# An adaLN, attention and mixture-of-experts block: the first large expert tiles are chosen from six batches and loaded ahead of the last sends

## The reference

```python
h = layernorm(x) * (1 + ca) + sa
x = x + ga * attention(h)             # exp(tanh(scores * 1/distance)), rows normalised
h = layernorm(x) * (1 + cb) + sb
logits = h @ Wg
top_v, top_i = top_k(logits, 2);  w = softmax(top_v)
sparse = sum over the two chosen e of  w_e * (relu(h @ W1[e] + b1[e]) @ W2[e] + b2[e])
shared = relu(h @ Ws1 + bs1) @ Ws2 + bs2
x = x + gb * (sparse + shared)
```

## Time and profile before

| | us |
|---|---|
| median of 3 runs | 648.14 (645.54 to 649.86) |
| profiled execution, its own time | 647.72 |
| its span | 646.0 |
| busy: PE / DVE / ACT / POOL | 609.2 / 461.2 / 402.3 / 345.7 |
| chain that ended last, PE's share | 66% |
| chain that ended last, POOL `rows_x` L577 | 5% |

### The profile page before, as it was taken

How to read it: one execution, slowest core, us unless ns; L and a number is a source line. 1 busy time by engine, 2 the same in 40 slices (tenths; PEclk the granted TensorE clock), 3 DMA queues, 4 the chain that set the end, 5 groups by cost and what they waited for, 6 DMA issues and landing times.

```text
span 646.0 us, 13359 instructions
## 1 busy us (share of the span) xinstructions
PE 609.2 (94%) x4311; PEld 555.7 (86%) x4311; DVE 461.2 (71%) x1403; ACT 402.3 (62%) x643; POOL 345.7 (54%) x341
## 2 busy tenths in 40 slices
PE   3898999999999998989988999999999999999995
PEld 2586988898889897878978999999999999999995
DVE  7889879798989898986812676765555445453788
ACT  3588787878787866567444556565555656555541
POOL 4531614766666666768660566666555556556000
PEclk9999999999999999989998999999999999999998
DMA  7140000111111111111256566666666666601972
GB/s 292 43 164 2 1 1 10 37 34 35 32 37 35 34 34 35 40 47 39 96 176 202 162 181 189 188 179 207 193 204 188 184 195 190 203 30 34 361 307 114
DMA packets 29885, 76.44 MB, mean 118 GB/s; under 512 B 7126, under 2 KB 11374, under 8 KB 29712
## 3 DMA queue, kind: packets, MB, share of 16 engines
q1 hardware_dynamic: 20480, 58.49, 28.1%
q0 software_dynamic: 8640, 16.93, 7.7%
q10 hardware_dynamic: 720, 0.47, 0.2%
HBM read 53.53 MB, written 23.24 MB: 119 GB/s over the span
## 4 chain that ended last, share of the span: by engine, by line
PE 66%; DVE 17%; POOL 7%; issue 6%; ACT 3%; DMA 1%; POOLq 0%; DVEq 0%; ACTq 0%; SPq 0%
PE value L1918 21%; PE value L1738 11%; PE score L1710 9%; PE score L1712 8%; PE score L1711 8%; POOL rows_x L577 5%; DVE rows_all L1168 2%; DVE stats L1039 2%; DVE rows_all L1155 2%; PE value L1969 2%; DVE work L1146 2%; PE misc L1751 2%; PE misc L1918 1%; PE misc L1693 1%; POOL rstd L557 1%
## 5 line engine op out<-in xcount | busy, mean ns | idle before, releaser
L745 POOL DMA_INDIRECT rows_z<-tile_y,tags x138 | 143.0, 1036 | 110.4 <-DVE tile_y L1535 49.7
L1710 PE MATMUL score<-h_hi,h_lo 128*128 128x512 f32 (+1 forms) x252 | 93.8, 372 | 2.5 <-DVE h_hi L1249 1.8
L1738 PE MATMUL value<-w_ring,work 128*128 128x129 f32 x768 | 93.6, 279 | 2.0 <-ACT work L805 1.9
L1738 PEld LDWEIGHTS value<-w_ring,work 128*128 128x128 f32 x768 | 91.2, 195 | 4.3 <-ACT work L805 2.6
L932 ACT ACTIVATE work<-score,w_ring 128x512 f32<-128x512 f32 (+1 forms) x96 | 53.1, 615 | 58.7 <-PE score L1712 57.1
L1712 PE MATMUL score<-h_hi,h_lo 128*128 128x512 f32 (+1 forms) x252 | 88.7, 352 | 0.0
L1711 PE MATMUL score<-h_hi,h_lo 128*128 128x512 f32 (+1 forms) x252 | 88.3, 351 | 0.0
L803 ACT ACTIVATE work<-work 128x1024 f32<-128x1024 f32 x64 | 67.2, 1050 | 26.9 <-DVE work L1146 26.7
L577 POOL DMA_INDIRECT rows_x<-work,slot x64 | 64.7, 1011 | 35.8 <-issue 17.7
L1146 DVE TENSOR_TENSOR work<-score,lw 128x1024 f32<-128x1024 f32 x64 | 76.5, 1214 | 1.8 <-PE score L1712 1.2
L1918 PE MATMUL value<-w_ring,work 128*128 128x128 f32 x640 | 75.4, 275 | 0.0
(11 more groups left out here) (253 smaller groups left out, 1216.3 us busy)
## 6 DMA issues: line engine op xcount, KB each, us to landing
w_ring<-packs SPq DMA_DIRECT2D x24, 578.0 KB, 3.8
rows_all<-packs SPq DMA_DIRECT2D x23, 578.0 KB, 3.9
lw<-rows_x SPq DMA_DIRECT2D x24, 260.0 KB, 3.6
res<-x SPq DMA_DIRECT2D x8, 512.0 KB, 5.9
h_t<-rows_z SPq DMA_DIRECT2D x3, 1024.0 KB, 9.9
mod<-mod_rows SPq DMA_DIRECT2D x1, 2560.0 KB, 10.0
rows_z<-tile_y,tags POOLq DMA_INDIRECT x142
rows_all<-rows_z SPq DMA_DIRECT2D x2, 1024.0 KB, 12.5
```

Of the source, the lines that this page charges most:

```text
L745: nc.gpsimd.indirect_dma_start(rows_z[:, :], bass.IndirectOffsetOnAxis(ap=tags[pos][:, k, 0:1].bitcast(I32), axis=0), tile_y[par][:, k, :] ...
L1710: nc.tensor.matmul(out, a_lo, b_hi, start=True, stop=False)
L1738: ins = nc.tensor.matmul(value[:, s // 3, c0:c0 + D + 1], prob[:, t % 4, s * P:(s + 1) * P], normal[b % 3][:, t, :], start=(t == 0 and s % ...
```

## The change

The first three large tiles of the table (positions 0, 2 and 4 of the first cycle) are always tiles of one expert: the one with most rows in batches 0 to 5. Three tiles are 1536 rows, which that expert has in these batches in any case, as 12288 rows go to 8 experts. `first_tiles`, ten small DVE instructions, picks it, fills the three entries and raises `first_ready`; the rest of the table is computed later for 21 large tiles, with that expert's region starting 1536 rows further and its count 1536 lower (one instruction more in `total_counts`). The number of tiles stays.

```diff
+            def first_tiles():
+                step = Chain(dve, chosen_step, 0)
+                step(nc.vector.tensor_tensor(count[:, :], place[:, 0, :], region_at[:, :], ALU.subtract))
+                step(nc.vector.max(first_v[:, :], count[:, :]))
+                step(nc.vector.max_index(first_i[:, :], first_v[:, :], count[:, :]))
+                step(nc.vector.tensor_copy(first_f[:, :], first_i[:, 0:1]))
+                step(nc.vector.tensor_tensor(first_hot[:, :], expert_no[:, 0, :], first_f[:, :].to_broadcast([P, E]), ALU.is_equal))
+                step(nc.vector.tensor_tensor(own_at[:, :], first_hot[:, :], region_at[:, :], ALU.mult))
+                step(nc.vector.tensor_reduce(first_r[:, :], own_at[:, :], AX.X, ALU.add))
+                step(nc.vector.tensor_copy(table_e[:, 0:RING, 0], first_f[:, :].to_broadcast([P, RING])), wait=False)
+                step(nc.vector.scalar_tensor_tensor(out=own_at[:, :], in0=first_hot[:, :], scalar=float(RING * TILE), in1=region_at[:, :],
+                                                    op0=ALU.mult, op1=ALU.add), wait=False)
+                nc.vector.tensor_scalar(table_r[:, 0:RING, 0], tile_no[:, 0:RING, 0], float(TILE), first_r[:, 0:1],
+                                        ALU.mult, ALU.add).then_inc(first_ready, 1)
+                dve.wait_ge(first_ready, 1)
+                dve.wait_ge(chosen_step, step.now())
```

DVE calls it between `split_x` of tile 3 and `last_rows`, and takes the `split_x` of tile 6 ahead of `small_tiles`:

```diff
             split_x(3, 1, shared_rows(3))
+            first_tiles()
             last_rows()
...
             large_tiles()
+            split_x(6, 0, shared_rows(6))
             small_tiles()
             small_table()
-            split_x(6, 0, shared_rows(6))
             split_x(7, 1, shared_rows(7))
```

SP loads W0 and W2 at `first_ready`, and R0 and R2 when the sends of six batches have landed, ahead of its wait for `counted` and of the pads; behind them only W1 and R1 are left:

```diff
+            sp.wait_ge(first_ready, 1)
+            for pos in range(0, RING, 2):
+                load_weights(pos, pos)
+            for par in range(2):
+                sp.wait_ge(scattered[par], 16 * 2 * G * FIRST_SENT // 2)
+            for pos in range(0, RING, 2):
+                load_rows(pos, pos)
+
             sp.wait_ge(counted, 1)
...
-            sp.wait_ge(large_table_ready, 1)
-            for pos in range(0, RING, 2):
-                load_weights(pos, pos)
             sp.wait_ge(table_ready, 1)
-            for pos in range(1, RING, 2):
-                load_weights(pos, pos)
-            rows_at = [first_row(pos, pos) for pos in range(RING)]
+            load_weights(1, 1)
+            row_at_1 = first_row(1, 1)
             sp.wait_ge(padded, 16 * (E + 1))
             for par in range(2):
                 sp.wait_ge(scattered[par], 16 * 2 * G * B // 2)
-            for pos in range(RING):
-                load_rows(pos, pos, rows_at[pos])
+            load_rows(1, 1, row_at_1)
```

PE's order becomes D5, U7, T0, D6, V0, wait `counted`, first half of D7, T1, second half of D7, T2, and then the loop as before:

```diff
             shared_up(7)
-            shared_down(6)
-            pe.wait_ge(counted, 1)
...
             transpose_rows(0, 0, True)
-            shared_down(FRONT - 1)
-            transpose_rows(0, 1, True)
+            shared_down(FRONT - 2)
             expert_up(0, 0)
+            pe.wait_ge(counted, 1)
+            shared_down(FRONT - 1, lambda: transpose_rows(0, 1, True))
             transpose_rows(0, 2)
```

ACT follows: the split of W0 comes ahead of `relu(7)`, the split of R0 ahead of the evacuation of D6, and that of D7 behind the split of R1:

```diff
             evacuate_shared(5)
-            relu(7, w_shared, 1)
-            evacuate_shared(6)
...
             expert_w(0, 0)
+            relu(FRONT - 1, w_shared, (FRONT - 1) % 2)
             expert_x(0, 0)
-            evacuate_shared(FRONT - 1)
+            evacuate_shared(FRONT - 2)
+            expert_relu(0, 0)
             expert_w(0, 1)
             expert_x(0, 1)
-            expert_relu(0, 0)
+            evacuate_shared(FRONT - 1)
             expert_w(0, 2)
```

More of the change, by code:

```diff
@@ L65 @@
 AHEAD = 3 + (B - 2) // 2
+FIRST_SENT = B - 2
+assert RING * TILE * E <= 2 * S * FIRST_SENT
+assert (LARGE_TILES - RING) * TILE <= 2 * T - RING * TILE - E * (TILE - 1) + TILE - 1
 assert LARGE_TILES * TILE <= 2 * T - E * (TILE - 1) + TILE - 1
@@ L209, in adaln_moe @@
         rest = sb("rest", [P, E])
+        first_v = sb("first_v", [P, E])
+        first_i = sb("first_i", [P, E], U32)
+        first_f = sb("first_f", [P, 1])
+        first_hot = sb("first_hot", [P, E])
+        first_r = sb("first_r", [P, 1])
+        own_at = sb("own_at", [P, E])
         count_i = sb("count_i", [P, E], I32)
@@ L326, in adaln_moe @@
         counted = sem("counted")
+        chosen_step = sem("chosen_step")
+        first_ready = sem("first_ready")
         large_table_ready = sem("large_table_ready")
@@ L1429, in tiles_up_to, with fill_table @@
                 return sum_of[3]
-            def fill_table(kind, ends, size, limit):
+            def first_tiles():
[14 more added lines that the diff above has]
+                dve.wait_ge(chosen_step, step.now())
+            def fill_table(kind, ends, size, limit, first=0):
                 tables(nc.vector.scalar_tensor_tensor(out=row_at[:, 0:E], in0=ends[:, before_], scalar=-float(size), in1=row_at[:, 0:E],
@@ L1435, in fill_table @@
                 tables(nc.vector.tensor_tensor(row_step[:, :], row_at[:, 1:E + 1], row_at[:, 0:E], ALU.subtract))
[L1437 to L1447, removed]
+                n = LARGE_TILES - first
+                ends_b = ends[:, own].rearrange("p (o e) -> p o e", o=1).to_broadcast([P, n, E])
+                step_b = row_step[:, :].rearrange("p (o e) -> p o e", o=1).to_broadcast([P, n, E])
+                tables(nc.vector.tensor_tensor(past[:, 0:n, :], tile_no[:, 0:n, :], ends_b, ALU.is_ge))
+                tables(nc.vector.tensor_reduce(tile_e[:, 0:n], past[:, 0:n, :], AX.X, ALU.add), wait=False)
+                tables(nc.vector.tensor_scalar(tile_r[:, 0:n], tile_no[:, 0:n, 0], float(size), row_at[:, 0:1], ALU.mult, ALU.add))
+                tables(nc.vector.tensor_scalar(table_e[:, first:, kind], tile_e[:, 0:n], float(E - 1), None, ALU.min), wait=False)
+                tables(nc.vector.tensor_tensor(past[:, 0:n, :], past[:, 0:n, :], step_b, ALU.mult))
+                tables(nc.vector.tensor_reduce(tile_e[:, 0:n], past[:, 0:n, :], AX.X, ALU.add))
+                tables(nc.vector.tensor_tensor(tile_r[:, 0:n], tile_r[:, 0:n], tile_e[:, 0:n], ALU.add))
+                return (nc.vector.tensor_scalar(table_r[:, first:, kind], tile_r[:, 0:n], float(limit), None, ALU.min))
             def total_counts():
@@ L1454, in total_counts @@
                 nc.vector.tensor_tensor(pad_at[:, :], count[:, :], region_at[:, :], ALU.add).then_inc(counted, 1)
+                dve.wait_ge(counted, 1)
+                tables(nc.vector.scalar_tensor_tensor(out=count[:, :], in0=first_hot[:, :], scalar=-float(RING * TILE), in1=count[:, :],
+                                                      op0=ALU.mult, op1=ALU.add))
             def large_tiles():
                 ends = tiles_up_to(0, count, TILE, 0)
-                tables(nc.vector.tensor_scalar(ends[:, own], ends[:, own], float(LARGE_TILES), None, ALU.min), wait=False)
-                tables(nc.vector.tensor_copy(row_at[:, 0:E], region_at[:, :]), wait=False)
+                tables(nc.vector.tensor_scalar(ends[:, own], ends[:, own], float(LARGE_TILES - RING), None, ALU.min), wait=False)
+                tables(nc.vector.tensor_copy(row_at[:, 0:E], own_at[:, :]), wait=False)
                 tables(nc.vector.memset(row_at[:, E:E + 1], float(SPARE)))
-                fill_table(0, ends, TILE, SPARE).then_inc(large_table_ready, 1)
+                fill_table(0, ends, TILE, SPARE, RING).then_inc(large_table_ready, 1)
                 dve.wait_ge(large_table_ready, 1)
                 tables(nc.vector.tensor_tensor(rest[:, :], ends[:, own], ends[:, before_], ALU.subtract))
-                tables(nc.vector.scalar_tensor_tensor(out=row_at[:, 0:E], in0=rest[:, :], scalar=float(TILE), in1=region_at[:, :],
+                tables(nc.vector.scalar_tensor_tensor(out=row_at[:, 0:E], in0=rest[:, :], scalar=float(TILE), in1=own_at[:, :],
                                                       op0=ALU.mult, op1=ALU.add), wait=False)
@@ L1908, in up, with down @@
                         ins.then_inc(up_ready, 1)
-            def down(n, w, bank, part, rows=TILE, first=False, banks=2):
+            def down(n, w, bank, part, rows=TILE, first=False, banks=2, halfway=None):
                 if not first:
@@ L1913, in down @@
                 for c in range(C):
+                    if halfway and c == PART:
+                        halfway()
                     if c % PART == 0:
@@ L1925, in shared_up, with shared_down @@
                 up(n, 0, n % 2, 0, first=(n == 0))
-            def shared_down(n):
-                down(n, w_shared, yacc[n % 2], n % 2, first=(n < 2))
+            def shared_down(n, halfway=None):
+                down(n, w_shared, yacc[n % 2], n % 2, first=(n < 2), halfway=halfway)
             def total_ranks():
```

## The result

The changed kernel takes 641.16 us (median of 5 runs, 640.41 to 642.41), the kernel before 647.41 (median of 5, 645.54 to 649.86): ratio 0.9911, 95% interval [0.9893, 0.9928], so 5.8 us less by the ratio. The profiled execution took 641.10 against 647.72, its span is 639.3 against 646.0. The forecast was 640.9. The change is real, but by the bound of 1% it falls into "within 1%", which I had given 0.43, and not into "faster by over 1%", to which I gave 0.53. The first four experiments (e1 to e4) fell in a time in which the kernel before took 674.8 us beside them, 28 more than otherwise, and why is open.

What follows compares the result with a forecast made beforehand. PE bounds the kernel, full in the expert loop with one idle hole ahead. Gains 6.75 + 0.65 - 0.24 = 7.16, taken as 7.2, off the profiled 647.72 give 640.5, or 640.9 against the median 648.14; range 638.8 to 645.0 us.

Steps and rivals of the forecast that it cites:

- within 1%: Total time: outcome that the change differs from the kernel before by less than 1% (6.5 us); chance 0.43.
- faster by over 1%: Total time: outcome below the 641.7 us line; chance 0.53, of which 0.50 forecast's case and 0.03 rivals.
- PE's order and the early loads: PE ahead of the expert loop: the same work without a wait takes 25.11 instead of 31.86 us, 6.75 gained.
- The low clock: PE behind its idle hole: first transposes and the `down` after them at low clock cost 1.73 us, part of 6.75.
- The loss in V1 and E0: Second expert `up` follows the first before ACT's ReLU is through: 5.70 instead of 5.22 us, 0.48 lost.
- `split_x` of tile 6: DVE: moved ahead of `small_tiles`, this split lets PE's `up` of tile 6 start at 323.48, 0.65 us gained.
- `first_tiles` at nothing: DVE: ten added instructions take 1.7 to 2.35 us and fit in 2.52 idle ahead of `last_rows`, costing nothing.
- the sends beside it would grow: Two sends beside `first_tiles` each grow by 0.98, together 2.0 us; part of a rival with chance 0.18.
- R1: Second tile's row load, behind the last send: its transposes on PE wait 0.24 us, range none to 1.5.
- R1 or the sends come late: Rival, ahead of the loop: late sends or row loads cut the gain to 4.1 or about 5.5 us; chance 0.18.
- the likeliest case: Total time: the forecast holds, with gains of 6.6 to 7.5 us, 639.0 to 642.7 with runs' spread; chance 0.67.
- Three quarters beyond the line: Share of the forecast's own case put past the 1% line at 641.7 us, giving 0.50.

Runs made afterwards that it cites:

- e1: Kernel before with only PE's and ACT's new order, first row load still behind all sends; ratio 1.0012, beside a kernel before at 674.8 us.
- e4: Kernel before with 38 useless matmuls filling PE's idle time ahead of the wait; ratio 1.013, beside a kernel before at 674.8 us.
- e2b: Changed kernel with PE's and ACT's order of the kernel before, early loads kept, second measurement; 641.18 us, ratio 0.9913 to the kernel before.
- e1b: Kernel before with only PE's and ACT's new order, no early loads, second measurement; 650.90 us, ratio 1.0061 to the kernel before.
- e4b: Kernel before with 38 useless matmuls filling PE's idle time ahead of the wait, second measurement; 649.65 us, ratio 1.0044.
- e6: Changed kernel with `split_x` of tile 6 moved back behind `small_table`; 640.49 us, ratio 0.9908 to the kernel before.
- c_after: Changed kernel measured again without any edit, as yardstick; 640.03 us, ratio 0.9907 to the kernel before.
- e5: Changed kernel with the second tile's transposes behind three quarters of the `down` around them instead of half; 640.18 us, ratio 0.99.
- e7: Changed kernel with one more POOL instruction, a useless power, ahead of the last three sends; 641.23 us, ratio 0.991 to the kernel before.
- e8: Changed kernel with 128 no-effect waits (64 instructions) on PE near the start, shifting its later code; 641.31 us, ratio 0.9915.

## Why the prediction was right

- **PE's order and the early loads (6.75).** Right in its working. The units hold: `down` 3.49, `up` 2.82, V1 with T3 and E0 5.23 instead of 5.22. e2b and e1b show what the text did not separate: the early loads carry 5.1 to 5.9 of 6.5, the order the rest, and the order by itself costs 3.6 to 3.9.
- **The low clock (1.73 of it).** Right; e4b gives 1.66.
- **The loss in V1 and E0 (0.48).** Right: present in e2b (5.69), gone in the changed kernel (5.23).
- **`split_x` of tile 6 (0.65).** Right in place (U6 at 323.43, forecast 323.48). Its worth in the sum is less sure: e6 lost 0.3 to 0.5 in the stretch by taking it back, of which 0.37 at U6 itself.
- **`first_tiles` at nothing.** Right: 1.87 us in an idle stretch, between my 1.7 and 2.35. `last_rows` came 0.2 later, which no one waited for (D4 starts at 319.94, before 319.99). That the sends beside it would grow did not come true: the undisturbed row is 1.26 apart there too, and the last send was issued 0.35 earlier than before. Nor does a long send belong to the instruction that ran beside it in the earlier trace rows (1.94 beside L1395): beside the same one, now L1409 at 302.09, a send took 0.96, and one of 1.97 came at 304.58.
- **R1 (0.24).** This term was mis-sized. I took R0's landing for R1's, which was fair (2.14 + 0.04 instead of 2.78 + 0.14), but I took the last send's landing of 2.28 as fixed. It was 3.85, and the stop at T1 cost 0.69 (0.55 in c_after). The sum's 7.16 became 6.52 to 6.66 in the profiles: 0.45 of the missing 0.64 is this, and the rest is spread thin (D7 with T1 3.79 in e5 where the sum has 3.69, V0 2.86 for 2.82, T0 and T2 together 0.80 for 0.76). Of the rival "R1 or the sends come late" this is the mild end, by a mechanism that I had not named: code for PE, loaded just when the last send comes.
- **The number.** That 641.16 lies so near to 640.9 is in part luck. The three runs of the kernel before, from which I counted, had a median of 648.14; the five have 647.41. Counted from these the forecast would be 640.2, and the likeliest case promised gains of 6.6 to 7.5, where the medians give 6.25.
- **The chances.** 1% lay 0.8 us inside my number. By the ratio the gain is 0.89%, 5.8 us, and the profiled executions differ by 6.6. Three quarters beyond the line was too much for a number that stood so near it.

## What to carry to other kernels

A stall on the engine that bounds the kernel can cost more than its length: here 4.5 us, and 1.7 more by the slow clock behind it (a stop of 0.8 in e7 left the clock at 1.00). Whoever takes it away gets both, and the loop behind keeps it. But work that is put ahead of a wait helps only if what is waited for really comes earlier: the same new order was worth 0.6 to 1.4 us with the early loads and cost 3.6 to 3.9 without them. When two chains have been made level, a term of one of them is no longer worth its face value, and the next tenths are in the landing of the last transfer and in what else shares its DMA engine.

## What the runs showed of the hardware

- An instruction load of 16 KB goes as one packet on one of the 16 DMA engines and takes it 1.17 us in the changed kernel, and a send that comes just then lands late, with 15 of its 16 parts long there. From the issue of the last send to that of the load behind it, which waits for its landing, it is 4.07 in the changed kernel, 4.02 in c_after, 4.08 in e5, 4.19 in e6, 3.88 in e4b and 3.48 in e2b, all with such a packet beside the send; 2.50 in the kernel before, 2.49 in e1b, 2.70 in e7 and 2.51 in e8, without one. Where it falls is set by how far PE is in its code: 64 added instructions moved it by 4.9 us.
- After 7.0 us without work (e1b) D6 took 5.75 at a granted clock of 0.61, after 4.3 us (before) D7 took 5.31, and with PE kept busy 3.7 at 1.00 (e4b).
